# A data-dependent loop of attention and feed-forward steps, reordered so that work moves by groups of four samples

## The reference, cut to what matters

```
def step(h, p):
    op = jnp.argmax(h[0, 0, :NOPS])
    q = h @ p['wq'][op]; k = h @ p['wk'][op]; v = h @ p['wv'][op]
    attn = jax.nn.softmax(jnp.einsum('bqd,bkd->bqk', q, k) * scale, axis=-1)
    y = jnp.einsum('bqk,bkd->bqd', attn, v) @ p['wo'][op]
    h = jnp.where(p['am'][op], y, h)
    z = jax.nn.relu(h @ p['w1'][op] + p['b1'][op]) @ p['w2'][op] + p['b2'][op]
    h = jnp.where(p['fm'][op], z, h)
    return (h, None)
out, _ = jax.lax.scan(step, x, xs)
```

## Time and profile before

| | us |
|---|---|
| median of 3 runs | 191.37 |
| lowest, highest | 190.82, 193.36 |
| span of the profiled execution | 191.5 |
| TensorE busy in it | 156.0 |
| VectorE, ScalarE, GpSimd busy | 113.1, 91.6, 63.1 |

### The profile page before, as it was taken

How to read it: one execution, slowest core, us unless ns; L and a number is a source line. 1 busy time by engine, 2 the same in 40 slices (tenths; PEclk the granted TensorE clock), 3 DMA queues, 4 the chain that set the end, 5 groups by cost and what they waited for, 6 DMA issues and landing times.

```text
span 191.5 us, 4344 instructions
## 1 busy us (share of the span) xinstructions
PE 156.0 (81%) x1443; PEld 97.0 (51%) x1447; DVE 113.1 (59%) x261; ACT 91.6 (48%) x183; POOL 63.1 (33%) x157
## 2 busy tenths in 40 slices
PE   7999997779906999997999877988956986898750
PEld 5879754334604556555543455655514564565310
DVE  1362668926996679649327265577663155587661
ACT  3563621416712244445325377686552448865740
POOL 2770000100451796800500064757000166754000
PEclk9999999978965799999655999999998599999995
DMA  5900000000000000001000000000010000000003
GB/s 151 334 9 0 0 3 3 0 0 3 3 0 0 2 3 0 3 0 26 3 0 9 18 0 3 0 3 2 3 26 2 0 0 0 0 0 0 0 0 113
DMA packets 3019, 3.48 MB, mean 18 GB/s; under 512 B 505, under 2 KB 2361, under 8 KB 3002
## 3 DMA queue, kind: packets, MB, share of 16 engines
q1 hardware_dynamic: 2858, 3.00, 5.1%
q10 hardware_dynamic: 144, 0.25, 0.4%
HBM read 2.73 MB, written 0.53 MB: 17 GB/s over the span
## 4 chain that ended last, share of the span: by engine, by line
PE 54%; DVE 24%; ACT 8%; issue 7%; POOL 3%; DVEq 2%; ACTq 0%; POOLq 0%
PE bank L568 7%; PE bank L550 6%; PE bank L636 6%; DVE sinv L1326 5%; PE bank L582 5%; PE bank L588 4%; ACT shifted L950 4%; DVE mem L1279 4%; PE bank L834 4%; PE bank L654 3%; PE bank L533 3%; PE bank L841 2%; PE bank L621 2%; POOL shifted L453 2%; PE bank L778 2%
## 5 line engine op out<-in xcount | busy, mean ns | idle before, releaser
L453 POOL TENSOR_SCALAR shifted<-shifted,nmax 128x256 f32<-128x256 f32 x96 | 44.8, 484 | 42.6 <-DVE nmax L1321 32.8
L963 ACT ACTIVATE big<-bank 128x512 f32<-128x512 f32 x48 | 27.6, 602 | 21.4 <-PE bank L568 21.4
L1321 DVE TENSOR_REDUCE nmax<-shifted 128x2 f32<-128x512 f32 x32 | 21.6, 684 | 22.5 <-ACT shifted L950 22.3
L568 PE MATMUL bank<-ident,shifted 128*128 128x128 f32 x192 | 26.9, 280 | 3.4 <-ACT big L963 2.7
L568 PEld LDWEIGHTS bank<-ident,shifted 128*128 128x128 f32 x192 | 20.5, 141 | 12.4 <-issue 8.0
L950 ACT ACTIVATE shifted<-bank 128x512 f32<-128x512 f32 x32 | 19.3, 604 | 9.7 <-PE bank L550 9.7
L1326 DVE RECIPROCAL sinv<-bank 128x256 f32<-128x256 f32 x12 | 21.0, 1751 | 3.1 <-PE bank L588 3.1
L1317 DVE CUSTOM_DVE_ANT_0 shifted<-bank,negm 128x256 f32<-128x256 f32 x32 | 11.3, 420 | 3.2 <-PE bank L550 3.1
L1101 ACT ACTIVATE big<-bank,wfs 128x512 f32<-128x512 f32 x16 | 9.9, 686 | 6.6 <-PE bank L834 6.6
L582 PE MATMUL bank<-big,v 128*32 128x256 f32 x192 | 12.9, 385 | 0.0
L588 PE MATMUL bank<-big,onesc 128*32 128x256 f32 x192 | 12.7, 381 | 0.0
(11 more groups left out here) (170 smaller groups left out, 230.1 us busy)
## 6 DMA issues: line engine op xcount, KB each, us to landing
xrev<-xrev_dram SPq DMA_DIRECT2D x1, 512.0 KB, 5.1
xin<-xtok_dram SPq DMA_DIRECT2D x1, 512.0 KB, 5.2
out_dram<-outT SPq DMA_DIRECT2D x2, 256.0 KB, 2.9
maskc<-maskc_dram SPq DMA_DIRECT2D x1, 256.0 KB, 5.2
kx<-kx_dram ACTq DMA_DIRECT2D x1, 248.0 KB, 3.0
wf<-wf_dram SPq DMA_DIRECT2D x3, 81.0 KB, 1.9
wx<-wx_dram SPq DMA_DIRECT2D x1, 216.0 KB, 4.1
constf<-constf_dram SPq DMA_DIRECT2D x1, 186.0 KB, 5.1
```

Source lines behind the costliest of these rows:

```text
L453: last = nc.gpsimd.tensor_scalar(sh[b % NSH][:, ih, :], sh[b % NSH][:, ih, :], -1.0 if masked else 1.0, nmax[:, b, ih:ih + 1], ALU.mult, A ...
L568: mm = pe.transpose(bank[4 + b % 2][:, jh * S + ih * P:jh * S + (ih + 1) * P], sh[b % NSH][:, ih, jh * P:(jh + 1) * P], ident)
L963: nc.scalar.activation(flat(probT[b]), bank[4 + b % 2][:, :], ACT.Exp).then_inc(s_P, 1)
L1321: m = nc.vector.tensor_reduce(nmax[:, b, :], sh[b % NSH][:, :, :], AX.X, ALU.max, negate=True)
```

## The change

The loop over steps is written anew on TensorE, ScalarE and VectorE, each with its own order, and with one counter per kind of work in place of the numbered tasks. What moves:

- Token 0, the choice of the next op, and the hidden strips of groups 0 and 1 move from behind the last turn into the attention, behind the normalisation of groups 0 and 1.
- Queries 1 to 3 and values 0 to 3 no longer stand ahead of quad 1; they are spread between turns and quads. All of them, the weight products and token 0 go through one bank, `TASKB` (bank 6); all weigh sums go through `SUMB` (bank 7).
- Turns 0 and 1 of a step move ahead of quad 1. In the groups after it quad g+1 comes behind turns 4g and 4g+1.
- The normalisation of group g moves on VectorE ahead of row maximum 4g+10 (g = 0) or 4g+11 (g = 1).
- The hidden strips of groups 2 and 3 are made one group at a time. If the next step attends, its weight products, queries 0 and 1, quad 0, values 0 and turns 0 and 1 stand between the outputs of this step ("merged" close).
- A kind 1 step waits for all four normed groups (before: for groups 0 and 1 first).
- GpSimd copies the feed-forward weights behind sample 5 (before: sample 10), after a wait for the whole state of the step before.
- The final additions to `outT` are made for each group by VectorE straight from PSUM; both stores wait for two groups each.

The diff, cut to its core:

```diff
@@ TensorE
+            def lead(att, a, d, gen):
+                weight_products()
...
+                queries(0)
+                pe.wait_ge(s_qA, a + 1)
+                quad(0)
+                queries(1)
+                pe.wait_ge(s_qA, a + 2)
+                values_of(0)
+                first_turns(att)
+            def attend(att, a, d, r, gen, rl, ffn):
+                wait(pe, s_cp, att, GB - B)
+                relus_drained(rl, 0)
+                quad(1)
+                pe.wait_ge(s_even, gen)
+                pe.wait_ge(s_vD, d + 1)
+                queries(2)
+                turn_pe(pe, att, 2)
+                pe.wait_ge(s_qA, a + 3)
+                pe.wait_ge(s_odd, gen)
+                values_of(1)
+                turn_pe(pe, att, 3)
+                pe.wait_ge(s_vA, d + 1)
+                queries(3)
+                turn_pe(pe, att, 4)
+                turn_pe(pe, att, 5)
+                wait(pe, s_cp, att, 2 * GB - B)
+                quad(2)
+                pe.wait_ge(s_qA, a + 4)
+                values_of(2)
+                pe.wait_ge(s_P, att + GB)
+                weigh(0)
+                turn_pe(pe, att, 6)
+                pe.wait_ge(s_vD, d + 2)
+                values_of(3)
+                turn_pe(pe, att, 7)
+                turn_pe(pe, att, 8)
+                turn_pe(pe, att, 9)
+                wait(pe, s_cp, att, 3 * GB - B)
+                quad(3)
...
+                    token0(TASKB)
+                    turn_pe(pe, att, 10)
+                    token0_row(TASKB)
...
+                weigh(1)
+                turn_pe(pe, att, 11)
+                turn_pe(pe, att, 12)
+                turn_pe(pe, att, 13)
+                pe.wait_ge(s_n, a + 2)
...
+                    hidden((0, 1, 2, 3), (0, 1))
+                pe.wait_ge(s_P, att + 3 * GB)
+                weigh(2)
+                turn_pe(pe, att, 14)
+                turn_pe(pe, att, 15)
+            def close(att, a, d, r, gen, rl, merged):
+                if merged:
+                    weight_products()
+                pe.wait_ge(s_n, a + 3)
+                relus_drained(rl, 2)
+                hidden((0, 1, 2, 3), (2,))
+                pe.wait_ge(s_P, att + B - 1)
+                output(0, 4)
+                pe.wait_ge(s_P, att + B)
+                weigh(3)
+                output(1, 5)
+                if merged:
...
+                    queries(0)
+                    relus_drained(rl, 4)
+                    output(2, 4)
+                    pe.wait_ge(s_qA, a + NG + 1)
+                    quad(0)
+                    pe.wait_ge(s_odd, gen + 1)
+                    queries(1)
+                    pe.wait_ge(s_qA, a + NG + 2)
+                    values_of(0)
+                    pe.wait_ge(s_cp, att + GB)
+                else:
+                    relus_drained(rl, 4)
+                    output(2, 6)
+                pe.wait_ge(s_n, a + 4)
+                hidden((0, 1, 2, 3), (3,))
+                if merged:
+                    pe.wait_ge(s_even, gen + 2)
+                    first_turns(att + B)
+                relus_drained(rl, 6)
+                output(3, 7)
@@ TensorE, kind 1
-                    pe.wait_ge(s_hlo, 2)
+                    pe.wait_ge(s_even, gen)
+                    pe.wait_ge(s_odd, gen)
@@ ScalarE, merged close
+                        hidden(hid + GB, (0, 1, 2, 3), (2,))
+                        state(z, 0, 4)
+                        exponential(att, 15)
+                        queries(a + NG, 0)
+                        state(z, 2, 4)
+                        for i in range(4):
+                            copy_scores(att + B, i)
+                        queries(a + NG, 1)
+                        hidden(hid + 2 * GB, (0, 1, 2, 3), (3,))
+                        exponential(att + B, 0)
+                        exponential(att + B, 1)
@@ VectorE, attend and merged close
+                for i in range(4, 10):
+                    row_max(att, i, False)
+                values_of(a, 0, 2)
+                normed_group(a, 0)
++                if ffn:
+                    pick_op(r, TASKB)
+                row_max(att, 14, False)
+                normed_group(a, 1)
+                row_max(att, 15, False)
+                if ffn:
+                    hidden(hid, (0, 1, 2, 3), (0, 1))
...
+                    normed_group(a, 2)
+                        weight_diagonals()
+                        hidden(hid + GB, (0, 1, 2, 3), (2,))
+                        normed_group(a, 3)
+                        state(z, 1, 5)
+                        row_max(att + B, 0, False)
+                        row_max(att + B, 1, False)
+                        values_of(a + NG, 0, 0)
+                        row_max(att + B, 2, False)
+                        hidden(hid + 2 * GB, (0, 1, 2, 3), (3,))
+                        row_max(att + B, 3, False)
+                        state(z, 3, 7)
```

More of the change, by code:

```diff
@@ L799, in _ @@
             scale(3)
-            def weight_products(into=PBANK):
-                pe.reg_alu(reg_next, reg_code, 2, ALU.bitwise_and)
-                with pe.If(pe.snap(reg_next) != 0):
-                    pe.reg_alu(reg_loads, reg_r, 16, ALU.mult)
-                    loads = pe.snap(reg_loads)
-                    pe.wait_ge(s_wA, loads)
-                    for i in range(2):
-                        pe.matmul(bank[into[i]][:, 0:P], wa[:, i * GB * C:(i + 1) * GB * C],
-                                  rep(wa[:, (2 * GB + i) * C:(2 * GB + i + 1) * C], NG), start=True, stop=True).then_inc(s_wp, 1)
@@ new lines, in hidden, with output @@
+            def hidden(banks, gs, before=None):
+                n = len(gs) * S
+                for q in range(GB):
+                    rows = slice(q * C, (q + 1) * C)
+                    if before and q == GB - 1:
+                        before()
+                    pe.matmul(bank[banks[q]][:, 0:n], w1r[rows, :], flat(hT[rows, gs[0]:gs[0] + len(gs), :]),
+                              start=True, stop=True, tile_position=(q * C, 0)).then_inc(s_hid, 1)
+            def output(g, into):
+                for q in range(GB):
+                    mm = pe.matmul(bank[into][q * C:(q + 1) * C, 0:S], w2s, relu[:, q, g, :],
+                                   start=True, stop=True, tile_position=(0, q * C))
+                mm.then_inc(s_z, 1)
@@ new lines, in hidden, with state @@
+            def hidden(at, banks, gs):
+                n = len(gs)
+                for q in (1, 3):
+                    dve.wait_ge(s_hid, at + (q + 1))
+                    nc.vector.tensor_scalar(relu[:, q, gs[0]:gs[0] + n, :],
+                                            bank[banks[q]][:, 0:n * S].rearrange("p (g s) -> p g s", g=n), b1s, 0.0,
+                                            ALU.add, ALU.max).then_inc(s_rD, 1)
+            def state(z, g, src):
+                dve.wait_ge(s_z, z + (g + 1))
+                nc.vector.tensor_scalar(hT[:, g, :], bank[src][:, 0:S], b2s, None, ALU.add).then_inc(s_odd, 1)
@@ L1424, in _ @@
+            dve.reg_alu(reg_next, reg_code, 2, ALU.bitwise_and)
+            with dve.If(dve.snap(reg_next) != 0):
+                lead(dve.snap(reg_att), dve.snap(reg_att4))
+            dve.reg_alu(reg_next, reg_code, 0, ALU.add)
             with dve.If(dve.snap(reg_code) >= NONE):
[L1425 to L1426 removed]
+                dve.wait_ge(s_even, 2)
+                dve.wait_ge(s_odd, 2)
                 add_state()
```

675 lines of the change are left out of this document (380 added, 295 removed).

## The result

Executions of one kernel differ by where the TensorE clock falls, and outlying ones are left out of the ratios. In every run that lists both numbers the time is 1.8 to 2.2 us more than the span, in most some 2.0.

The account below looks back on a forecast made before the run. TensorE was taken as the nearest bound, 3.3 us to spare in the middle. The walk, with 3.58 us storing and 0.7 for the feed-forward step, gave 192.0; one clock fall of 2.4 made 194.4 us; range 187.5 to 198.5.

Parts of the forecast that it names:

- Rival 2: Clock falls two or three times, around 140 to 150 and near 178: 196.8 or 199.2 us; chance 0.22.
- The walk of the loop: Each engine's list followed in order with trace prices: 192.0 us in all if the clock stays at 2.4 GHz.
- quad 1 to weigh 3: First attention step, middle into merged close: weigh 3 some 28 us behind quad 1, at 142.33 instead of 137.37.
- weigh 3 to the next quad 1: Merged close into the second attention step: weigh 3 at 142.33, next quad 1 at 152.76, 10.43 us.
- the last step: Second attention step to the end: output 3 at 186.52, last addition ends at 187.7 us, before at 187.92.
- rival 3: Idle time in the middle and last step does fill, no clock fall: 185.5 us; chance 0.16.
- the period: From quad 1 to quad 1 of the next step: 38.44 us, against 38.7 before at full clock.
- Exponential 15: Closes, ScalarE: starts 3 us after its turn, behind two relus and group 0's state, and holds weigh 3.
- The feed-forward step: Kind 1 step waits for the fourth normed group: everything after it 0.7 us later (bounds 0.4 and 1.1).
- The lead: Stage up to quad 1: 0.7 us won, despite 1.9 us idle before values 0 behind the single bank.
- Output 3 to the next quad 1: End of the merged close: 152.23 to 152.76 us, 0.53 us, the price of an output.
- The number of falls: Clock falls in the new kernel: one forecast, at 2.4 us, taking 192.0 to 194.4.

Follow-up runs that it names:

- e12: Kernel after, order and waits untouched, with empty products in the loop, behind output 3 and ahead of the loop; 189.79 us, ratio 0.990.
- e3: Kernel after with exponential 15 moved ahead of group 2's relus and group 0's state on ScalarE in both closes; 193.53 us, ratio 1.012.
- e5: Kernel after with kind 1's wait split: token 0 and first strips start after three normed groups, the fourth is awaited later; 195.16 us, ratio 1.006.
- e1: Kernel after run again without any edit; median 194.82 us, 1.0% above the kernel before.
- e6: Kernel after with query 1 written to SUMB in the lead and the merged close; 194.38 us, ratio 1.010.
- e9: Kernel after with the edits of e3, e5, e6 and e8 together; 188.08 us, ratio 0.989.
- e10: Kernel before with e7's empty products and 2 + 4 more in the norm ahead of the loop; 185.57 us, ratio 0.974.
- e4: Kernel after without the code for kind 2 steps (attention only), which the data never enter; 196.62 us, ratio 1.032.
- e8: Kernel after with TensorE's five register updates moved ahead of the close; 197.08 us.
- e7: Kernel before with empty products in two idle stretches of the tail (4 before the block diagonals, 5 before outputs 2 and 3); 189.95 us, ratio 0.987.
- e11: e9 with empty products in the loop, behind output 3 and ahead of the loop; 184.83 us, ratio 0.972.
- e2: Kernel after with empty products in TensorE's idle stretches of the lead and both closes; 194.43 us, ratio 1.016.

## Why the prediction came out as it did

**The median lies in the range, and near the forecast for a reason that is partly luck.** The forecast was 194.4 us; the two medians of the kernel after are 197.25 and 194.82. The base of the sum was wrong: the text ahead of the prediction says that nothing lies around the span, while time and span differ by some 2.0 us in every run that lists both. By that offset the profiled 191.5 us belong to an execution of about 193.4 us, near the slowest of that kernel, and not to the median. The forecast, made against a span, was thus one of 196.4 us in time. As a change it was +2.9 us; the medians moved by +5.5 in the first set and +1.9 in the second. Rival 2 gave spans of 196.8 and 199.2, and the profiled execution has 199.1 with three falls up to the last output; that match is luck, since the three falls together cost 5.3 us and not 7.2 (below).

**The walk of the loop** was right in its sum at full clock, with errors that partly cancel. From quad 1 to the last output it gave 33.76 + 38.44 = 72.2 us; e12 took 72.69. Its parts: quad 1 to weigh 3 in 28.0 us, measured 27.33 to 27.48; weigh 3 to the next quad 1 in 10.43, measured 12.33; the last step in 33.76, measured 33.03. The middle is indeed longer than the old 22.36 by the products and waits moved into it, so the idle time did not fill (rival 3 is out: 185.5), and the period, which was to be 38 to 39 us, is 39.66 at full clock; the old order's, put at 38.7 in the prediction, is 39.75 with the empty products and some 39.1 without. So the comparison held to half a microsecond: what the overlap wins the middle gives back.

**Exponential 15** was put 3 us behind its turn; it began at 143.30, 3.3 us behind the end of turn 15 (140.01). e3 prices it: 2.3 us over the two closes. **The feed-forward step** was put at 0.7 us and cost 0.77 at the strips; e5 takes it back. In the first execution it came to 1.9 us up to the weight products; the clock rose at 108.9 us there instead of 105.6.

**The lead** was forecast 0.7 us shorter. It was, by 0.4 us in the profiled execution (7.99 against 8.41) and by 0.53 in e1 (112.79 - 104.91 = 7.88). The 1.9 us idle behind the one bank was there as 1.78, but was not worth that much: turn 0 waits for GpSimd's sample 0, which is there only 0.4 us earlier, as e6 shows, and with two banks quad 1 is no earlier (e9: 112.50 - 104.28 = 8.22 us from the weight products). In the merged close the same bank costs 1.3 us.

**Output 3 to the next quad 1: the step that failed in the walk.** It was put at 0.53 us, the price of an output, and took 2.49 in the kernel after. The passage between two steps had no row of its own in the walk. The old order has such a passage too: in e10 2.63 us from the last relu to the next step's first product, of which the weight products and the second pair of outputs cover all but 0.86 us. In the kernel before the block diagonals end at about the same moment (146.78), so that its profile names them and not the passage. e4 rules out the code of the steps that never run, and e8 all but 0.1 to 0.2 us of the register updates. What else makes up the 2.4 us stays open.

**The number of falls was the largest mis-sized term.** The forecast put one fall at 2.4 us. The profiled execution has three after 110 us; from quad 1 to the last output it is 78.0 us against 72.69 at full clock (e12), 5.3 us of low clock. The old order lost 70.87 - 69.01 (e10: 178.03 - 109.02) = 1.9 us to its one, or nearly 2.5 if the 0.6 us of e10's own empty products are taken off, which fits the 2.4 forecast. But a fall has no fixed price: e1's one, 3.4 us long, cost at most 73.12 - 72.69 = 0.4 us; under it TensorE's idle time before quad 1 shrank from 1.85 us to 0.91, so that most of the slower work fell into a wait. The places named for rival 2, the merged close and the last one, are where two of the three falls came; the third stands at 160.1, just behind quad 1 of the second step. The rule quoted from the Trainium skill (TensorE: Matmul & The Clock Gate, "A second HAM failure mode: psum-queue depth-cycling") fits the fall at 143: from quad 1 on (116.48) no idle stretch of TensorE ahead of it was over 0.87 us, it was a series of short ones. That idle stretches are behind the falls of the loop is shown by filling them: the profiles of e7, e10, e11 and e12 have none between the first quad 1 and the last output, and that of e2 only one, where nothing was filled; of the profiles of unfilled lists all but that of e9 have at least one. Which fall comes is another matter: with the same waits one execution (e1) had one short fall there where the other had three, and e9 had none with nothing filled.

**The sum of the loss.** Of the 7.1 us between quad 1 and the last output, 72.69 - 69.01 = 3.7 are the order's and 3.4 the clock's; with the 0.6 us of e10's empty products taken off it is 4.3 and 2.8. The order's part is nearly all in the last step (33.03 against 29.26). Some 2.1 us of that are work that the old list has ahead of quad 1 and the new one behind it (by the prediction's prices, 3.2 us of queries and values, less 1.1 for turns 0 and 1), and 1.0 us is exponential 15. In the first step the merged close pays for the moved work; that the last step can't, since nothing of a next step is there to overlap with, is argued and not tested. Mended (e9, e11) the new order is level with the old one, 77.20 to 77.55 us from the weight products on (some 76.9 for the old one without its empty products), and as a whole 0.972 to 0.974 with both filled. So the loss is that of the waits that the new list brings; but the idea wins nothing measurable over the old list at full clock. What e10 and e11 win, 2.6% and 2.8%, is in the main the clock's.

**Open.** e9 is 9.2 us below the first median of the kernel after (6.7 below the second), and by stages at equal clock only 80.6 - 77.37 (e9: 181.65 - 104.28) + 0.77 = 4.0. The rest would be falls that no longer come, whether by the edits or by chance (its trace has none from 103.3 to 181.8); that was seen in one execution, and what decides in which execution the clock falls where was not found. The two medians of the kernel after also lie 2.4 us apart, and e2, e3, e5 and e6 have intervals that reach about 1, so that each edit's worth rests on its stage in the trace.

## What to carry to other kernels

Walking each engine's list in order with prices from the trace foretold 73 us of a reordered loop to half a microsecond at full clock, in part because errors of up to 1.9 us in single stages cancelled; give the passage from one loop turn to the next, and what lies around the span, a row of their own. Look in every engine's list for work that others wait for and that stands behind work nobody waits for (exponential 15 behind the relus, one drain behind four copies). Where the clock falls in some executions, compare orders by stages at equal clock, and try first to fill TensorE's short idle stretches with empty products, looking in the trace whether they hold real work back (0.6 us in one place here): that gave 2.6% in the old order, and the mended reordering alone 1.1%.

## What the runs showed of the hardware beyond this

One program had spans of 190.7 and 199.1 us with the same work in its stages, by the number and the place of the falls. The clock fell at 143 with no idle stretch over 0.87 us in the 26 us ahead. A fall cost from at most 0.4 us (e1, 3.4 us long) to about 2.5 (the kernel before, 6.8 us long). Once low, the clock stayed so while TensorE was busy for 8.68 of 8.90 us (the window from 99.59). With six empty products ahead of the loop a low stretch of 13.6 us was gone in the profiles of e10 and e11, but one of 6.8 us stood in that of e12. From the end of the last relu that TensorE waited for to the first product of the next turn of the loop it took 2.4 to 2.8 us in both orders, whatever stood between (an output of 0.5 us, or two of 1.0 and the weight products).
